# Graph block with two attentions, one core: the linear attention's pairs placed between the groups of the two graph aggregations

## What is computed

```
xn  = layernorm(x)
# graph network, two layers, 8 relations; layer 2 takes relu(layer 1)
msg = segment_mean(xn[src], by dst and edge type);  h = sum_r msg_r @ W1[r] + xn @ root1 + b1
# linear attention, 12 heads of 64 (= 6 pairs of heads), 256 random features
q, k, v = split(xn @ W_qkv);  phi(t) = exp(t @ F.T - 0.5*|t|^2) / 16
kv  = phi(k).T @ v ;  out = (phi(q) @ kv) / (phi(q) @ sum(phi(k)) + 1e-6)
mix = layernorm(xn + out @ W_proj + b_proj) * gamma + beta
x   = x + gnn + mix
x   = x + experts_attention(layernorm(x))
```

## Time and profile before

| | us |
|---|---|
| median of three runs | 3312.5 (3307.17 to 3315.47) |
| the profiled execution, its own time | 3310.68 |
| span of its records | 3308.9 |
| first aggregation, from its first gather to its last | 600.5 to about 1034 |
| second aggregation, the same | 1550.1 to about 1962 |
| linear attention, six turns | about 1998 to 2387 |
| join, first to last row | about 2405 to 2510 |

### The profile page before, as it was taken

One profiled execution on the slowest core, in us unless ns is written; L12 is line 12 of the kernel. 1 busy time (PEld: TensorE's weight loads), 2 busy tenths in 40 slices (PEclk: granted clock), 3 DMA queues, 4 the chain that ended last, 5 costly groups with the idle time before them and its releaser, 6 DMA issues.

```text
span 3308.9 us, 66031 instructions
## 1 busy us (share of the span) xinstructions
PE 2769.4 (84%) x22935; PEld 2024.6 (61%) x22935; DVE 1577.5 (48%) x2801; ACT 783.9 (24%) x1105; POOL 1277.4 (39%) x1388
## 2 busy tenths in 40 slices
PE   6998999765555999999755558999986999999999
PEld 5787888454444788886544446777654555555555
DVE  7576666633334333234333322333487566557551
ACT  2211113000000221212000004544312545554540
POOL 2683111377774000002777751000141534643562
PEclk9999999885555999999865559999997999999999
DMA  4333433599996223233999982000241000000003
GB/s 150 103 102 114 148 120 120 176 313 312 311 313 207 85 94 122 94 117 126 306 316 311 314 307 70 14 14 19 64 119 38 1 20 20 20 1 20 20 30 98
DMA packets 101064, 434.20 MB, mean 131 GB/s; under 512 B 19721, under 2 KB 20044, under 8 KB 96641
## 3 DMA queue, kind: packets, MB, share of 16 engines
q0 software_dynamic: 55712, 266.88, 23.9%
q1 hardware_dynamic: 42417, 124.07, 11.8%
q10 hardware_dynamic: 2736, 40.50, 3.5%
HBM read 354.46 MB, written 76.88 MB: 130 GB/s over the span
## 4 chain that ended last, share of the span: by engine, by line
PE 56%; POOL 15%; DVE 11%; issue 10%; DMA 3%; DVEq 2%; ACT 2%; SPq 0%; POOLq 0%; ACTq 0%
PE PS L1614 24%; POOL GATA L618 7%; PE PS L1955 5%; POOL ROW L618 4%; PE PS L1772 3%; PE PS L1623 3%; PE PS L1885 3%; POOL MSG L618 2%; PE PS L1780 2%; DVE NMC L1535 2%; PE PS L1942 2%; PE PS L1817 2%; PE PS L1801 2%; PE PS L1943 2%; PE PS L1791 2%
## 5 line engine op out<-in xcount | busy, mean ns | idle before, releaser
L1614 PE MATMUL PS<-WHL,XT 128*125 (+1 forms) x2880 | 487.5, 329 | 7.0 <-DVE WHL L1030 4.2
L1614 PE MATMUL PS<-WHL,HT 128*125 (+1 forms) x2880 | 476.9, 329 | 12.0 <-DVE HT L1183 9.4
L1614 PEld LDWEIGHTS PS<-WHL,HT 128*125 (+1 forms) x2880 | 395.2, 138 | 90.1 <-DVE HT L1183 10.6
L1614 PEld LDWEIGHTS PS<-WHL,XT 128*125 (+1 forms) x2880 | 391.0, 138 | 83.0 <-issue 4.6
L672 POOL TENSOR_TENSOR PL<-PF 125x500 bf16<-125x500 f32 (+1 forms) x360 | 322.4, 932 | 214.6 <-ACT PF L887 213.8
L618 POOL DMA_INDIRECT GATA<-msg_table,SKEY x324 | 310.3, 958 | 116.0 <-issue 95.2
L1739 PE MATMUL PS<-HOT,GATA 128*128 128x64 f16 x1944 | 180.2, 209 | 184.3 <-DMA GATA<-msg_table,SKEY 153.0
L1117 DVE SCALAR_TENSOR_TENSOR MSG<-PS,MSG 125x768 f16<-125x768 f32 x160 | 153.1, 957 | 360.7 <-ACT MSG L711 358.8
L711 ACT ACTIVATE MSG<-PS 125x768 f16<-125x768 f32 x160 | 129.7, 811 | 794.5 <-PE PS L1614 794.5
L1739 PEld LDWEIGHTS PS<-HOT,GATA 128*128 128x128 f16 x1944 | 149.9, 118 | 211.1 <-DMA GATA<-msg_table,SKEY 97.7
L1955 PE MATMUL PS<-PF,V 125*128 125x500 bf16 (+1 forms) x720 | 242.8, 350 | 16.0 <-POOL PL L672 14.1
(11 more groups left out here) (305 smaller groups left out, 4960.6 us busy)
## 6 DMA issues: line engine op xcount, KB each, us to landing
msg_table<-MSG SPq DMA_DIRECT2D x160, 336.0 KB
WST<-in_wg_dram ACTq DMA_DIRECT2D x16, 2304.0 KB, 10.1
WST<-in_wf_dram SPq DMA_DIRECT2D x7, 1536.0 KB, 6.5
KROW<-key_rows POOLq DMA_DIRECT2D x54, 192.0 KB, 3.8
msg_table<-MSG SPq DMA_DIRECT2D x160, 39.0 KB
WST<-in_wm_dram SPq DMA_DIRECT2D x5, 1152.0 KB, 5.2
GATA<-msg_table,SKEY POOLq DMA_INDIRECT x324, 4.7
ROW<-msg_table,SKEY POOLq DMA_INDIRECT x216
```

The lines of the kernel that those rows point to most:

```text
L1614: ins = pe.matmul(PS[0:ROWS, b0 + h, 0:HALF], X[:, xp, k, bass.ts(t, ROWS)], panel_part(slot, wp, k, h), start=k == 0 and xp + wp == 0, st ...
```

## The change

The loop over the six pairs is gone. Three pairs are worked through inside each aggregation. `behind_groups(L)` deals the results of `MIX` (now k, v, K, kv for both heads, then q, Q and o) out over the groups by a count of columns, 6900 to a group; the root pieces now stand one behind each of the first 12 groups, and the pairs fill groups 12 to 72 (with the last pair's division in 74 to 76). TensorE works off the entry of a group right after that group's pass, ScalarE only the entries that concern it, and VectorE the entry of group g after the `take_pass` of group g, that is, inside the iteration of group g + 1. The entries are, beside the results of `MIX`: R a root piece; X, T, Y, B, Z the search for the largest weight of a pair (X on VectorE, T and B on TensorE, Y and Z on VectorE), H and L its split on ScalarE and VectorE; D0 to D2 the division, in three parts.

Weights of a pair are split in place, into the upper half of `WST` (`WMX`). q and k share one buffer, KP and QP one place (that of `HT`), and VA, KV, RCP, NUM lie where slot 0 of `WHL` is. Only banks 3 to 6 of `PS` are used. The column of ones in VA is one column instead of 64, so kv has 65 columns for each half instead of 128, and VectorE copies the sum to 64 columns afterwards. A pair's result is divided in `NUM`, stored to `hf_rows` in DRAM, and read back to `HF` when TensorE is through with the last pair; the sixth stays in `NUM`. `WPR` is loaded during the second aggregation. The weights for the experts' gate (`W_LORA`) are split after the second aggregation. Four semaphores with which engines count their own loop steps became one (`tick`).

```diff
+        def behind_groups(L):
+            first, pieces = LPAIRS * L, len(PIECES) - ROOT_FIRST
+            slots = [[] for _ in range(AG + 1)]
+            for n_ in range(pieces):
+                slots[n_].append(("R", ROOT_FIRST + n_))
+            for n_, ahead in enumerate(("X", "TY", "BZ", "H", "L")):
+                slots[n_ + 3] += [(x, first) for x in ahead]
+            grp, columns = pieces, 0
+            for i in range(first, first + LPAIRS):
+                for r, _ in MIX:
+                    if i + 1 < first + LPAIRS and r in AHEAD:
+                        slots[grp] += [(x, i + 1) for x in AHEAD[r]]
+                    slots[grp].append((r, i))
+                    if i > first and r in ("k0", "k1", "k2"):
+                        slots[grp].append((f"D{r[1]}", i - 1))
+                    columns += mix_columns(r)
+                    if columns >= BEHIND * (grp - pieces + 1) and grp < AG - 1:
+                        grp += 1
...
-        mix = Order([(r, e, (i % 8,)) for i, (r, e) in enumerate(MIX)], "mix")
+        mix = Order([(r, e, (3 + i % MIX_BANKS,)) for i, (r, e) in enumerate(MIX)], "mix")
...
 # SyncE
+                first = LPAIRS * L
+                sp.wait_ge(S["w_lo"], REL + 2 if L == 0 else W_GNN)
+                pair_weights(first)
+                if L == 1:
+                    sp.wait_ge(S["root_done"], 2 * len(PIECES))
+                    sp.dma_start(WPR[:], a["wmp"]).then_inc(S["wp_in"], 16)
...
+            pair_out(4)
+            sp.wait_ge(S["mix_pe"], mix.made(PAIRS - 1, "o12"))
+            sp.wait_ge(S["hf_out"], 16 * (PAIRS - 1))
+            for i in range(PAIRS - 1):
+                sp.dma_start(HF[:, i, :], hf_rows[i * 128:(i + 1) * 128, :]).then_inc(S["hf_in"], 16)
...
 # VectorE
+                    elif r[0] == "o":
+                        h, (c0, n) = int(r[1]), CHUNKS[int(r[2])]
+                        v.wait_ge(S["mix_pe"], mix.made(i, r))
...
+                        v.tensor_scalar(RCP[64 * h:64 * h + 64, c0:c0 + n], PS[64:128, b, 0:n], 1e-6, None, ALU.add)
+                        v.tensor_copy(NUM[64 * h:64 * h + 64, c0:c0 + n], PS[0:64, b, 0:n]).then_inc(S["mix_dve"], 1)
+                    else:
+                        c0, n = CHUNKS[int(r[1])]
+                        v.drain()
+                        v.reciprocal(RCP[:, c0:c0 + n], RCP[:, c0:c0 + n])
+                        v.drain()
+                        v.tensor_tensor(NUM[:, c0:c0 + n], NUM[:, c0:c0 + n], RCP[:, c0:c0 + n], ALU.mult).then_inc(S["hf_made"], 1)
...
-                    if grp % 2 == 0 and grp and r < len(PIECES):
-                        take_root(r)
-                        r += 1
+                    if grp:
+                        behind(grp - 1)
                 take_pass()
+                behind(AG - 1)
+                behind(AG)
...
 # TensorE, at the end of a group
                     pe.matmul(PS[:, 7, 320:322], ZERO[:, 0:128], ZERO[:, 0:2], start=True, stop=True).then_inc(S["group_read"], 1)
-                    if grp % 2 and r < len(PIECES):
-                        root_piece(r)
-                        r += 1
+                    behind(grp)
...
-            with pe.Fori(0, PAIRS) as it:
...
+            pe.wait_ge(S["hf_made"], 3 * PAIRS)
+            pe.wait_ge(S["hf_in"], 16 * (PAIRS - 1))
```

408 lines of the change are left out of this document (233 added, 175 removed).

## The result

The changed kernel takes 2973.2 us (median of 4 runs, 2969.1 to 2982.9) against 3314.0 for the kernel before (4 runs, 3307.2 to 3319.3): a ratio of 0.898, 95% interval 0.895 to 0.901. Timed once more beside its last experiment it took 2975.5 (5 runs), ratio 0.898 (0.897 to 0.899). Forecast were 2956, in a range of 2922 to 3020: the side, the range and the case were right, and the time itself 17 us too low.

The account below looks back on a forecast made before the run. Aggregations wait for data, paced by GpSimd's gathers at 5.03 us a group; linear attention waits for TensorE. 3310.7 - 404.3 (stage removed) + 36 (aggregations) + 12 (transfers) = 2954.4, plus 1.8 for the median: 2956 us, range 2922 to 3020.

Parts of the forecast that it names:

- the side: Whole kernel: faster than the kernel before by more than about 0.3% (10 us), chance 0.96.
- the case: Whole kernel: the forecast itself, 2956 us, own range 2935 to 2990, chance 0.61, against hidden, VectorE-bound and slower rivals.
- the sums by stage: Aggregations: per pair TensorE needs 92 us and VectorE 94.6 of the 102 that 20.3 groups give.
- the mean share of the engines: Aggregation transfers: DMA share 0.91 leaves 37 of 407 us free, so added loads fit; plus 2 and 10 us taken.

Follow-up runs that it names:

- its last experiment: Changed kernel plus search moved to q products, alternating root pieces, WPR in six pieces, the 14120-column group parted: 2954.0 us, ratio 0.891 against the kernel before.
- top_twice: Changed kernel with VectorE's reduction for each pair's largest weight (2304 columns, one input in SBUF) made twice in a row: 3005.0 us.

## What to carry to other kernels

When one stage is laid behind the groups of another, sum each engine per group and not per stage: an operation of the second engine belongs beside a piece of the first that is long enough to cover it, and a move of a few entries by that rule, with long and short root pieces in turn, one overfull group parted, and one load cut in pieces and parted from its neighbour, was worth 21 us where the sums by stage showed nothing. Price a load beside a paced gather by the delay of its burst, against the lateness that the buffers let pass in the changed kernel, where each group is read later than before, and not by the mean share of the engines. Look too at which other load leaves with it. A gain ahead of the next bad place may be lost there: mend the places together, and time them together.

## What the runs showed of the hardware

- TensorE's clock fell to 0.5 in the midst of a stage in which it is 91% busy. The falls that were followed up came behind waits of 2 us and more, as after 1.80 us busy in 5 (0.58 in the next 7), where the fall doubled the price of the wait.
- An operation on VectorE of 2304 columns with two inputs in SBUF holds the issue of one indirect gather on GpSimd to 2.2 to 3.3 us; a reduction of the same columns does not (0.94 to 0.96 us in top_twice), and a product of 500 hardly does (mostly 0.95, at most 1.45).
- Beside a burst of 3456 KB on SyncE's queue the two queues moved about as many packets (222 and 208), and the gathers, with the smaller packets, a third of their usual bytes.
- Float32 products of 65 columns behind 128-column weights come every 276 ns, like those of 128 columns.
- GpSimd stood 2.0 us with no releaser shown at group 28 and 1.3 to 2.0 at group 79 of the second aggregation in every profile of the changed kernel, and not before the change. What it does there stays open.
